# A decoder's delta-rule attention re-staged: diagonal blocks turned last and with 128 columns, GpSimd subtracting, VectorE keeping a solved piece, and smaller edits before and behind it

## The reference, cut to what matters

```
x = ln(x + L0_attn(x))            # softmax attention, 4 queries a key head, with an elu(q)+1 memory read
x = ln(x + L0_xattn(x, ctx))      # cross-attention over channels, rotary positions
x = ln(x + L0_ffn(x))             # top-2 of 8 experts
x = ln(x + L1_attn(x))            # delta rule, then causal softmax attention
x = ln(x + L1_xattn(x, ctx, mask))# masked cross-attention, clipped scores, own layernorm of the delta
x = ln(x + L1_ffn(x))             # 8 fused experts and a shared one
```

```
# L1_attn, 16 heads of 16:
q = rope(x @ Wq); k = rope(l2norm(x @ Wk)); v = x @ Wv; beta = 2 * sigmoid(x @ Wb)
A = tril((k k^T) * beta_j, -1)                 # 64 x 64 for each head
v = solve_triangular(eye + A, v)               # in 4 chunks of 16 tokens here
out = softmax(causal(q (k*beta)^T / 4)) @ v @ Wo
# L1_xattn, 16 heads of 16:
delta = clip(residual_scale, 0, 0.3) * (softmax(clip(q k^T / 4), mask) @ v @ Wo^T + bo)
delta = (delta - mean) / sqrt(var + 1e-5) * ln_gamma + ln_beta
```

## Time and profile before

| | us |
|---|---|
| three runs | 1006.14, 1008.82, 1010.19 |
| median | 1008.82 |
| the profiled execution | 1011.24 |
| its span (first to last instruction) | 1009.4 |
| TensorE busy | 943.3 |
| VectorE busy | 526.8 |
| ScalarE busy | 372.7 |
| GpSimd busy | 206.3 |

### The profile page before, as it was taken

One profiled execution on the slowest core, in us unless ns is written; L12 is line 12 of the kernel. 1 busy time (PEld: TensorE's weight loads), 2 busy tenths in 40 slices (PEclk: granted clock), 3 DMA queues, 4 the chain that ended last, 5 costly groups with the idle time before them and its releaser, 6 DMA issues.

```text
span 1009.4 us, 19505 instructions
## 1 busy us (share of the span) xinstructions
PE 943.3 (93%) x7768; PEld 608.2 (60%) x7768; DVE 526.8 (52%) x1062; ACT 372.7 (37%) x778; POOL 206.3 (20%) x254
## 2 busy tenths in 40 slices
PE   9999899999899999999888898888899999999995
PEld 4765543333359999997457687756554554554553
DVE  2689788898451110102882787868643232233235
ACT  2434536676623323233475378243330000000002
POOL 6021100000021322212144901830101121112111
PEclk9979999999999999999997799999799999999998
DMA  6000320000156555643241401130114113323001
GB/s 216 2 2 1 142 121 2 2 2 2 40 196 253 175 192 174 193 158 122 104 49 23 127 1 40 48 151 2 52 33 112 50 46 95 95 95 95 1 1 42
DMA packets 28843, 82.18 MB, mean 81 GB/s; under 512 B 10188, under 2 KB 17516, under 8 KB 22692
## 3 DMA queue, kind: packets, MB, share of 16 engines
q1 hardware_dynamic: 26548, 74.91, 22.8%
q0 software_dynamic: 2208, 6.03, 1.9%
HBM read 70.65 MB, written 8.55 MB: 78 GB/s over the span
## 4 chain that ended last, share of the span: by engine, by line
PE 62%; DVE 22%; issue 8%; ACT 3%; DMA 3%; SPq 1%; POOL 0%; DVEq 0%; ACTq 0%; POOLq 0%
PE psum L1219 8%; PE psum L1231 8%; DVE arena L2273 5%; PE psum L1662 5%; PE psum L1462 3%; PE psum L1650 3%; PE psum L924 3%; PE psum L1694 2%; PE psum L1628 2%; PE psum L1108 2%; PE psum L1666 2%; DVE arena L2190 2%; DVE arena L2189 2%; PE psum L1698 1%; PE psum L1391 1%
## 5 line engine op out<-in xcount | busy, mean ns | idle before, releaser
L2121 ACT ACTIVATE arena<-psum 128x512 f32<-128x512 f32 (+1 forms) x32 | 19.0, 595 | 216.2 <-PE psum L1666 216.2
L1922 ACT ACTIVATE arena<-psum,arena 128x128 f32<-128x128 f32 x184 | 52.6, 368 | 109.3 <-PE psum L1219 68.7
L2273 DVE TENSOR_REDUCE arena<-psum 128x2 f32<-128x512 f32 x128 | 82.4, 688 | 13.3 <-PE psum L1054 11.9
L1662 PE MATMUL psum<-arena 128*128 128x512 f32 (+1 forms) x192 | 89.2, 599 | 0.0
L848 POOL TENSOR_TENSOR arena<-arena 128x512 f32<-128x512 f32 (+1 forms) x32 | 40.6, 1270 | 229.4 <-ACT arena L2121 229.4
L1219 PE MATMUL psum<-arena 128*128 128x128 f32 x736 | 86.0, 275 | 0.3 <-ACT arena L1914 0.3
L1219 PEld LDWEIGHTS psum<-arena 128*128 128x128 f32 x736 | 84.1, 192 | 0.6 <-ACT arena L1914 0.6
L1231 PE MATMUL psum<-arena 128*128 x368 | 83.3, 380 | 0.0
L2717 DVE TENSOR_TENSOR arena<-psum,arena 128x512 f32<-128x512 f32 x32 | 22.1, 692 | 111.7 <-issue 99.8
L1899 ACT ACTIVATE arena<-psum 128x1024 f32<-128x1024 f32 x64 | 65.5, 1026 | 33.2 <-PE psum L1076 30.0
L2416 DVE COPY arena<-psum 128x256 f32<-128x256 f32 x23 | 9.8, 425 | 122.6 <-PE psum L1198 122.6
(11 more groups left out here) (365 smaller groups left out, 1778.4 us busy)
## 6 DMA issues: line engine op xcount, KB each, us to landing
arena<-in_w SPq DMA_DIRECT2D x31, 1024.0 KB, 8.9
arena<-in_experts SPq DMA_DIRECT2D x8, 1248.0 KB, 6.5
arena<-mixed SPq DMA_DIRECT2D x16, 256.0 KB
arena<-mixed SPq DMA_DIRECT2D x8, 512.0 KB, 9.0
arena<-returned SPq DMA_DIRECT2D x8, 256.0 KB, 5.0
kept<-arena SPq DMA_DIRECT2D x2, 1024.0 KB, 7.9
arena<-kept SPq DMA_DIRECT2D x2, 1024.0 KB, 6.6
arena<-arena SPq DMA_DIRECT2D x11, 128.0 KB, 4.7
```

The costliest lines, as they stand in the source:

```text
L1662: pe.matmul(out, e[w][:, k, :], xe6[:, half, k, :], start=(k == 0), stop=False)
L1922: last = act.activation(hidt[:, r % 2, ic * P:(ic + 1) * P], bank(n)[:, i * P:(i + 1) * P], ACT.Gelu, bias=b1_tile[:, r % 4, ic:ic + 1])
L2273: ax_max.by(dve.tensor_reduce(nmx[:, b % 2, :, h], bank(u % 2).rearrange("p (t s) -> p t s", t=2), AX.X, ALU.max, negate=True))
```

## The change: what it does

- L0: ScalarE's `exp(q0)` moves from tile 7 of its loop to tile 5, VectorE's elu from tile 7 to tile 6, which puts it ahead of `rope_x(7)`.
- L1 projections: ScalarE's copy of q and k is gone; VectorE's rotary instructions read PSUM, in two pairs of buffers, and GpSimd adds the halves. VectorE's square sum waits for the square alone. Tile j + 2 of the projection waits until the rotary instructions have read tile j. One of the three instructions on beta is folded into another.
- Both diagonal turns stand behind the key loop, back to back, in banks 4 to 7 and 0 to 3, with the moving operand repeated to 128 columns; the `keep_clock` between them is gone. ScalarE's copies become four of 256 columns.
- The solve takes the groups in the order 2, 3, 0, 1 (VectorE's half of the inverses first), SyncE returns that half first. From step 2 on GpSimd makes the difference of the scores; its copies of units for chunks 2 and 3 become eight of 1024 columns, one ahead of each of its first eight subtractions. VectorE copies one solved piece in four. The wait for all raw scores stands behind the first `rest_of_chunk`. A `keep_clock` of four passes stands behind the last solved piece.
- L1 cross-attention: `wo` is scaled once, the bias is added by a bfloat16 matmul (96 rows holding three parts of it), and VectorE's scaling instruction is gone; its statistics read PSUM. Tiles 6 and 7 use banks 2 and 4. Nine small VectorE instructions prepare this.
- Behind it: ScalarE normalises tiles 0 to 3, and VectorE's order there is changed.

The diff, cut to its core:

```
-        turn_a, turn_b = (kp1[:, 0, k, 0:2 * D] for k in range(KC))
+        turns1 = [[kp1[:, e, k, 0:2 * D] for k in range(KC)] for e in range(2)]
-        FIRST_TURN = 24
+        POOL_FROM = 2
-            return xv1.rearrange("p (s m q) x -> p s m q x", s=GROUPS, q=4)[:, t % GROUPS, :, q, :]
+            return xv1.rearrange("p (s m q) x -> p s m q x", s=GROUPS, q=4)[:, GROUP_ORDER[t % GROUPS], :, q, :]
...
# SyncE
-            for g in range(2):
+            for g in (1, 0):
...
# GpSimd
+            for j in range(NT):
+                pool.wait_ge(rope_read.sem, rope_read.base + j + 1)
+                rope_done.by(pool.tensor_tensor(out=qk1[:, j, :], in0=turns1[j % 2][0], in1=turns1[j % 2][1], op=ALU.add))
...
-            for chunk in (2, 3):
-                rows = slice(32 * chunk, 32 * chunk + 32)
-                do(pool.tensor_copy(na1[rows, chunk, :, :]...
+            for n in range(POOL_FROM, 2 * NT):
+                if n < POOL_FROM + 2 * GROUPS:
+                    chunk, group = divmod(n - POOL_FROM + 2 * GROUPS, GROUPS)
...
+                    do(pool.tensor_copy(na1[rows, chunk, units, :]...
+                pool.wait_ge(mx_ready.sem, mx_ready.base + n - POOL_FROM + 1)
+                pool.wait_ge(pt_ps.sem, n - 1)
...
+                do(pool.tensor_tensor(out=sm, in0=raw1(W_ORDER[n]).rearrange("p (h t) -> p h t", t=S),
+                                      in1=wide(mx1[:, n % 2, :], 2, S), op=ALU.subtract), sm_pool)
...
# TensorE
+                    pe.wait_ge(rope_read.sem, rope_read.base + j - 1)
...
-                    last = pe.matmul(bank(banks[i // 8])[:, i % 8 * S:(i % 8 + 1) * S], rows[:, g * P:(g + 1) * P, i],
-                                     in_order1, start=True, stop=True, skip_group_check=True)
+                    last = pe.matmul(bank(banks[i // 4])[:, i % 4 * P:(i % 4 + 1) * P], rows[:, g * P:(g + 1) * P, i],
+                                     wide(in_order1, 1, 2), start=True, stop=True, skip_group_check=True)
...
-                if j == FIRST_TURN // 4:
...
-                    turn_diagonal(0, [n % 6 for n in range(FIRST_TURN, FIRST_TURN + 2)])
-            keep_clock(2, 6)
+            pe.wait_ge(gather_dma.sem, gather_dma.base + 48)
+            pe.wait_ge(ti1_blank.sem, ti1_blank.base + 1)
+            pe.wait_ge(na_dve.sem, na_dve.base + 2 * (NT - 1))
+            turn_diagonal(0, range(4, 8))
...
+            turn_diagonal(1, range(4))
...
-            pe.wait_ge(raw_sb.sem, raw_sb.base + 2 * NT)
             for t in range(SOLVES + 1):
                 if t < SOLVES:
                     rest_of_chunk(t)
+                if t == 0:
+                    pe.wait_ge(raw_sb.sem, raw_sb.base + 2 * NT)
...
+            keep_clock(2, 2)
...
+                pe.matmul(sum_bank5(j)[:, 0:D], each5[0:96, :], thirds5[0:96, :], start=True, stop=False)
...
# ScalarE
-                if u == 7:
+                if u == 5:
                     act.wait_ge(q_sb.sem, 6)
                     elu_exp.by(act.activation(sig0, q0, ACT.Exp))
...
-                act.activation(qk1[:, j, :], bank(2 + 2 * (j % 2)), ACT.Copy)
...
-                for q in range(4):
+                for q in range(3):
                     xv_act.by(act.activation(group_units(t, q)[32 * chunk:32 * chunk + CH],
...
+            act.wait_ge(less_mean.sem, 4)
+            for j in range(4):
+                normalise_x([j])
...
# VectorE
-                if u == 7:
+                if u == 6:
                     dve.wait_ge(elu_exp.sem, 1)
...
-                do(dve.tensor_tensor(out=qk1[:, j, :], in0=turn_a, in1=turn_b, op=ALU.add))
...
             for t in range(SOLVES):
                 own_heads(t)
+                if t >= 1:
+                    keep_last_solved(t - 1)
...
-                do(dve.scalar_tensor_tensor(out=delta5[:, j, :], in0=bank(1)[:, 0:D],
-                                            scalar=scale5[:, 0:1], in1=bo5, op0=ALU.mult, op1=ALU.add), y5_read)
-                do(dve.bn_stats(stats[:, j, :], delta5[:, j, :]))
+                do(dve.bn_stats(stats[:, j, :], sum_bank5(j)[:, 0:D]))
```

More of the change, by code:

```diff
@@ L2585, in _ @@
             do(dve.tensor_scalar(bo5, x1["bo"], scale5[:, 0:1], None, ALU.mult))
+            do(dve.tensor_scalar(x1["wo"], x1["wo"], scale5[:, 0:1], None, ALU.mult))
+            do(dve.memset(each5, 1.0 / 32))
+            do(dve.tensor_copy(thirds5[0:96, :], bo5[0:96, :]))
+            for first in (32, 64):
+                for at in range(first, 96, 32):
+                    rows = slice(at, at + 32)
+                    do(dve.tensor_tensor(out=bo5[rows, :], in0=bo5[rows, :], in1=thirds5[rows, :], op=ALU.subtract))
+                    do(dve.tensor_copy(thirds5[rows, :], bo5[rows, :]))
             def divide5(j):
```

164 lines of the change are left out of this document (100 added, 64 removed).

## The result

| | before | after |
|---|---|---|
| median of six runs, us | 1006.77 (1004.92 to 1010.19) | 998.54 (990.83 to 1000.15) |
| profiled execution, us | 1011.24 | 998.00 |
| its span | 1009.4 | 996.1 |

The ratio is 0.9884, with a 95% interval of 0.9855 to 0.9913: faster by 1.2%, 993.0 forecast and 998.5 measured, inside the range of 983 to 1003. The gain in medians is 8.2 us, where the forecast had 15.8 (1008.82 to 993). The six times lie in two lots, four from 998.0 to 1000.2 and two at 990.8 and 991.3. The profiled execution of the kernel before (1011.24) is 4.5 above the median of its six times and the one after (998.00) is close to its own, so that differences between the two traces, 13.3 us in all, are larger than what the change gives as a rule.

A forecast was written before the change was run, and what follows sets the result against it. TensorE, busy 93% of the span, was taken to bound the kernel. Terms +2.1 - 13.6 - 5.0 = -16.5 took 1011.24 to 994.7, as a median 992.3, stated as 993; range 983 to 1003, about 8 in 10.

The forecast's parts named there:

- L0: Elu ahead of the last rotary step: TensorE idles 4.1 us before the last replication, net +2.1, upper end 5.
- The clock term: L0, clock fall after the idle stretch: replication up to 4.00 instead of 2.00, products behind too, up to 2.6.
- Projections: L1 projections: the 0.71 wait for VectorE before the head turns goes, -0.65; +1.2 if the new wait stalls tiles.
- Turns: Two diagonal turns behind the key loop: 7.19 us each, wider stream costs nothing, 535.5 to 549.9; bounds 9.0 and 3.5.
- The round trip of the inverses: After VectorE's inversion: through HBM to TensorE at about 569, estimated some 8 us.
- Third turn: Probabilities' third turn in the solve: bounded by GpSimd's first difference, at 574.7; -12.9 from projections to here.
- Solve: Solve steps: stay 2.94, cost 0; GpSimd needs 2.3, then 1.27; VectorE's 3.90 subtraction beside GpSimd's copies goes.
- The middle together: Projections through end of solve: -12.9 and -0.7 make -13.6, with ends at -8 and -20.
- Rival 4: Solve: GpSimd's subtraction becomes the bound, steps of 4.9 then 3.9, +21.4, giving 1014; chance 0.04.
- rival 2: Turns of 5 or so, or the clock stays up through turns, scores and norms: 987; chance 0.15.
- rival 3: Half the middle's gain goes: turns of 9.0 (+3.5), scores at clock 0.50 (+2.4), elu (+3): 1000; chance 0.28.
- Cross-attention and behind: L1 cross-attention tiles 3.5 instead of 3.87 (-2.8), last norms about 2.2 shorter: -5.0, bounds -2 and -9.

The follow-up runs named there:

- elu_behind: Changed kernel with VectorE's elu back behind rope_x(7) and stack_x(6), ScalarE's exponential left at tile 5: 985.46 us, ratio 0.9781.
- before_elu_early: Kernel before with only the exponential moved to tile 5 and the elu to tile 6: 1015.50 us over 12 runs, ratio 1.0070.
- after: The changed kernel itself, all edits against the kernel before: median 998.54 us, profiled execution 998.00 us, ratio 0.9884.
- after_again: The changed kernel run once more, nothing changed: 995.94 us, ratio 0.9879.

## Why the prediction was right where it was, and wrong in one step

The time lay in the range, and the direction and most mechanisms were right. The gain was forecast at 16.5 and came to 13.3 between the profiled executions, and was forecast at 15.8 and came to 8.2 between the medians. One step failed by 5.7; the others together gave 2.5 more than said, which hid part of it.

- **L0, wrong.** The step said "+2.1", with 5 as its upper end. Measured +7.8 in the profiled execution; alone in the kernel before, +7.1 of medians; taken out of the changed kernel, 5.4 of medians. The wait was right (4.1 said, 4.13 measured), and its net price nearly so: +2.3 by the rows. The clock term was mis-sized: the forecast left it out of the +2.1 and let the fall cost the replication and "the products behind" up to 2.6 at the upper end, but it lasted 23 us, in which the replication took 3.79 and `memory0`'s 32 passes 3.68 instead of 2.00 each. I bounded it by the first instructions behind the wait. The upper end was also added up wrongly: with nothing of the wait given back, my own terms make 3.6 + 2.6 = 6.2, not 5. The Trainium skill's rule ("TensorE: Matmul & The Clock Gate", Part 1), that the throttled clock is the default and activity releases it, spoke for the upper end, and the trace agrees with it in sign (0.50 behind the wait). How soon activity releases it is another matter: TensorE was busy 2.00 of every 2 us for over 20 us before the clock came back.
- **Projections.** -0.65 said, -1.2 measured. The wait of 0.71 went, as said; the other half is nowhere forecast.
- **Turns.** 14.4 said, 14.25 measured (64 passes; the forecast's last paragraph writes 32 by a slip). The Trainium skill's other rule ("TensorE: Matmul & The Clock Gate", Part 3, The mechanism), by which weights load beside running matmuls only where row groups differ, would have had 18; here 128 columns in place of 64 changed nothing, so the columns do lie beside a load. The cause I gave, the stride, is shown by the dense weights. The round trip of the inverses, which the forecast put at some 8 us with no row behind it, is 8.5 in `elu_behind`, where the first solved piece waits for it.
- **Third turn.** 574.7 said, from turns that start at 535.5, 39.2 later; measured 38.5 (542.62 to 581.16). The step's own terms end at 573.6, which would be 38.1; the 1.1 up to 574.7 and the 0.2 "taken as spare" have no row behind them and were not needed. GpSimd is the bound there, as said, and the time pays for everything put ahead of its first difference. This difference takes 1.04, less than the 1.27 borrowed from the experts' product of the same shape.
- **Solve.** Steps of 2.94 said, 2.93 measured. That VectorE had to be relieved is shown by the 3.36 without it: I had named the change's benefit there the freed 3.90, and this was the wrong one. The 3.90 was one instruction; VectorE would have bounded each step once it also keeps a piece.
- **The middle together** -13.6 said, -15.0 measured. Three copies instead of four at the end gave 0.8 (0.7 said). Rival 4 is out: GpSimd's subtraction is not slower. Of rival 2 the faster turns are out, but its clock that stays up through turns and scores came true. Of rival 3 one part came true, the elu, at about twice its +3 (7.8 for 2.1); the turns of 9.0 and the scores at clock 0.50 did not.
- **Cross-attention and behind.** -5.0 said, -6.1 measured: a tile 3.5 said, 3.49 measured; norms "by 712 plus the shifts", that is -5 relative to the stage before, measured 705.98 after a shift of -7.2, so -3.8, and another 2.3 at the router and the first experts' products, where the clock is at 0.50 from about 713 to 727 us before and from 707 to 713 after. That share was not forecast.

What stays open is why some executions of the changed kernel are 8 us shorter (a higher clock goes with it, but no profile of one was had), and what decides how long a fall lasts.

## What to carry to other kernels

When an instruction is moved ahead of one that TensorE waits for, price the wait and then the clock behind it, for as long as falls are seen to last and not for the next instruction alone. Here a wait of 4.1 us, priced at 2.1, cost 5 to 8 against the old order and 10 or more against the better one. If the wait can't go, idle matmuls in it can pay where the fall would be a long one, even when they are longer than the wait. Read an edit's worth in the stage that it touches, since the clock in unchanged code moves the total by as much as most edits. And before a stage is made faster (here, the turns), follow the other engine's queue to the same meeting point, for the gain ends where that one becomes late.

## What the runs showed of the hardware that was not expected

- After one and the same wait of 4.13 us the granted clock was back after some 4 us in one execution (`before_elu_early`) and after some 23 and 25 in two others (`after`, `after_again`), with TensorE busy all through in all three.
- Weights read 16 elements apart cost 0.22 us a pass, consecutive ones 0.12 (128x128, float32, 128 moving columns).
- In unchanged code of about 420 us, profiled executions of kernels with small edits elsewhere differed by up to 6.2 us, and in the two furthest apart the time at clock 0.50 differed by some 20 us.
- GpSimd's difference of 128x512 takes 1.04 us against 1.27 for its product of the same size in the experts (L870); VectorE's, beside GpSimd's copies of 1024 columns, takes up to 1.11 instead of 0.69.
